# Shared expert of a two-layer AdaLN model: gate and up projections with the weights stationary, and a new order of the dense stage

## The reference

```python
logits = x @ W_gate_router
scores = jax.nn.sigmoid(logits)
_, sel = jax.lax.top_k(scores + expert_bias, 2)
top_scores = take(scores, sel); top_scores = top_scores / top_scores.sum(-1)
shared = (silu(x @ Wg_s) * (x @ Wu_s)) @ Wd_s          # x: 4096x256, Wg_s and Wu_s: 256x192, Wd_s: 192x256
h = silu(x @ Wg[e]) * (x @ Wu[e])                      # eight experts of the same size, two of them for a token
out = shared + sum over the two chosen experts of top_score * (h @ Wd[e])
```

## Time and profile before

| what | value |
| --- | --- |
| runs (us) | 916.97, 918.64, 922.68 |
| median (us) | 918.64 |
| span of the profiled execution (us) | 911.5 |
| dense stage in that execution (us from the span's start) | 338.4 to about 477 |
| PE busy over the span | 831.9 us, 91% |
| DVE, ACT, POOL busy over the span | 72%, 52%, 42% |

### The profile page before, as it was taken

The page is one execution under the profiler, slowest core; times in us unless marked ns, Lnnn a source line. Parts: engine busy times, 40 slices in busy tenths (PEclk is TensorE's granted clock), DMA queues, the critical chain, the costliest instruction groups (busy, mean ns, idle before and its releaser), DMA issues.

```text
span 911.5 us, 16937 instructions
## 1 busy us (share of the span) xinstructions
PE 831.9 (91%) x5115; PEld 744.7 (82%) x5115; DVE 652.8 (72%) x1917; ACT 474.6 (52%) x1006; POOL 379.5 (42%) x427
## 2 busy tenths in 40 slices
PE   6899999999999978889868999999698899988997
PEld 5789998987999877778758999999577788876776
DVE  3666677735567676878784676576768999888986
ACT  2443343434334338777724676466344345449883
POOL 3542200169000014564642445475678886423230
PEclk9799999989999995999998999999899999999999
DMA  9200000000000004242335445334411200000112
GB/s 306 104 1 1 2 1 1 2 1 1 1 1 1 2 22 136 89 140 89 112 112 148 126 129 179 103 112 133 128 47 47 65 29 1 1 1 24 47 47 70
DMA packets 47799, 58.31 MB, mean 64 GB/s; under 512 B 5599, under 2 KB 42848, under 8 KB 47712
## 3 DMA queue, kind: packets, MB, share of 16 engines
q1 hardware_dynamic: 39856, 39.11, 14.5%
q0 software_dynamic: 6480, 16.92, 5.1%
q10 hardware_dynamic: 1376, 1.20, 0.4%
HBM read 34.91 MB, written 23.22 MB: 64 GB/s over the span
## 4 chain that ended last, share of the span: by engine, by line
PE 32%; DVE 15%; issue 6%; ACT 5%; POOL 2%; SPq 1%; DMA 0%; DVEq 0%; ACTq 0%; POOLq 0%
PE bank L80 7%; PE bank L82 7%; PE bank L81 7%; PE bank L1701 2%; PE bank L1709 2%; PE bank L1600 1%; DVE xm L2090 1%; PE bank L1717 1%; PE bank L1721 1%; PE bank L1718 1%; PE bank L1719 1%; PE bank L1720 1%; DVE st L2026 1%; ACT spare L1211 1%; DVE hth L1415 1%
## 5 line engine op out<-in xcount | busy, mean ns | idle before, releaser
L367 ACT CAST pth<-tp 128x512 fp32r<-128x512 f32 (+3 forms) x80 | 41.7, 525 | 128.8 <-PE tp L717 127.4
L1144 POOL DMA_INDIRECT results<-row_tiles,idu x71 | 70.0, 986 | 89.0 <-ACT row_tiles L1293 75.0
L1128 POOL DMA_INDIRECT region<-row_tiles,posu x64 | 66.3, 1035 | 59.8 <-DVE posu L1399 42.7
L547 DVE TENSOR_TENSOR ptl<-tp,pth 128x512 fp32r<-128x512 f32 (+3 forms) x80 | 48.2, 607 | 54.7 <-ACT pth L367 54.6
L80 PE MATMUL cx<-vh,pth 128*128 128x256 f32 x272 | 80.6, 296 | 1.4 <-DVE ptl L547 1.2
L82 PE MATMUL cx<-vh,ptl 128*128 128x256 f32 x272 | 76.8, 282 | 0.0
L81 PE MATMUL cx<-vl,pth 128*128 128x256 f32 x272 | 76.8, 282 | 0.0
L80 PE MATMUL sc<-hh,ph 128*128 128x512 f32 (+3 forms) x160 | 61.0, 381 | 0.3
L82 PE MATMUL sc<-hh,pl 128*128 128x512 f32 (+3 forms) x160 | 58.3, 364 | 0.0
L81 PE MATMUL sc<-hl,ph 128*128 128x512 f32 (+3 forms) x160 | 58.1, 363 | 0.0
L358 ACT ACTIVATE prob<-sc,nmx 128x512 f32<-128x512 f32 (+3 forms) x80 | 49.4, 628 | 14.0 <-DVE nmx L520 14.0
(11 more groups left out here) (430 smaller groups left out, 2787.0 us busy)
## 6 DMA issues: line engine op xcount, KB each, us to landing
row_tiles<-region SPq DMA_DIRECT2D x71, 130.0 KB, 2.3
pairs_a<-results SPq DMA_DIRECT2D x10, 512.0 KB
x<-in_x SPq DMA_DIRECT2D x8, 512.0 KB, 10.7
out<-x SPq DMA_DIRECT2D x8, 512.0 KB, 2.9
pairs_b<-results SPq DMA_DIRECT2D x6, 512.0 KB, 4.9
early<-in_wmod SPq DMA_DIRECT2D x2, 768.0 KB, 4.6
early<-in_wmod SPq DMA_DIRECT2D x1, 1536.0 KB, 8.3
spare<-in_wg SPq DMA_DIRECT2D x8, 192.0 KB, 2.7
```

What stands on the lines that cost most here:

```text
L367: a_.copy(pth[:, m % 2, 0:w], tp[:, m % 2, 0:w]).then_inc(s["pt_hi"], 1)
L547: vec.tensor_tensor(ptl[:, m % 2, 0:w], tp[:, m % 2, 0:w], pth[:, m % 2, 0:w], ALU.subtract).then_inc(s["pt_lo"], 1)
L1128: g_.indirect_dma_start(region, bass.IndirectOffsetOnAxis(ap=posu[:, c, t:t + 1], axis=0), hb[:, G % HB, j], None).then_inc(scattered[G % ...
L1144: g_.indirect_dma_start(results, bass.IndirectOffsetOnAxis(ap=idu[:, j % 8:j % 8 + 1], axis=0), y[:, j % YR, 0:D], None, bounds_check=KS * ...
```

## The change

The shared expert no longer goes by tile but by group and feature-major: the gate and up weights are the stationary operand and the 512 tokens of a group stream through (`dense_up(G, m)`, three blocks m of 128 features, 6 matmuls of 512 columns each). The 192 features of gate and of up are laid out by the host as features 128 to 191 of gate and of up (block 0), features 0 to 127 of gate (block 1), the same of up (block 2); the two weight inputs become one array `wgu_s`. The gated values come out feature-major, as the down product needs them, so that `turn`, `ht_hi`, `ht_lo` and `hidden` go from this stage. In their place come, per group, two silus, two products, three copies for the high part and two subtractions, on 512 columns each; the down product (`dense_down`) keeps its 20 matmuls, in two halves of two tiles that share one PSUM bank, and the sum to x is added by halves (512 columns).

The arrays `fh` (high parts) and `fl` (low parts) have one copy each, and `act2` too. The lists of the four engines are written anew, one pass of the loop per group:

```diff
+            def gate_b(G):
+                act.wait_ge(g["up_ready"], G * 3 + 1)
+                need(act, g["lo"], G * 2 - 1)
+                a_.activation(act2[F - P:P, 1], up3[0:F - P, 0], ACT.Silu).then_inc(g["silu_done"], 1)
+            def gate_a(G):
+                act.wait_ge(g["up_ready"], G * 3 + 2)
+                need(act, g["lo"], G * 2)
+                a_.activation(act2[:, 0], up3[:, 1], ACT.Silu).then_inc(g["silu_done"], 1)
+            def hi_b(G):
+                act.wait_ge(g["product"], G * 2 + 1)
+                need(act, g["down_ready"], G * 2)
+                a_.copy(fh[F - P:P, 1], act2[F - P:P, 1]).then_inc(g["hi"], 1)
+                a_.copy(fh[0:F - P, 1], act2[F - P:P, 1]).then_inc(g["hi"], 1)
+            def hi_a(G):
+                act.wait_ge(g["product"], G * 2 + 2)
+                need(act, g["down_ready"], G * 2)
+                a_.copy(fh[:, 0], act2[:, 0]).then_inc(g["hi"], 1)
...
             for G in range(1, GROUPS + 1):
+                gate_b(G - 1)
                 if G < GROUPS:
+                    h_hi(G)
                     sigmoid(G)
+                hi_b(G - 1)
+                if G + 1 < GROUPS:
+                    z_of(G + 1)
+                gate_a(G - 1)
                 if G < GROUPS:
                     h_back(G, 0)
+                    up_weights(G + 1, G)
+                    h_back(G, 1)
+                hi_a(G - 1)
                 if G + 1 < GROUPS:
+                    h_of(G + 1)
                 if G < GROUPS:
                     down_weights(G + 1, G)
...
+            for G in range(1, GROUPS):
+                product_b(G - 1)
+                h_lo(G)
+                if G > 1:
+                    add(G - 2, 0)
+                choose(G)
+                low_b(G - 1)
+                if G > 1:
+                    add(G - 2, 1)
+                weigh(G)
+                low_up_weights(G + 1, G)
+                product_a(G - 1)
+                rank_of(G)
+                low_a(G - 1)
+                low_down_weights(G + 1, G)
...
+            def dense_up(G, m):
+                need(pe, g["product"], G * 2 - 1 if m == 0 else G * 2)
+                for e in range(KC):
+                    last = three(nc.tensor, up3[:, m], gsh[:, e, q], gsl[:, e, q], hh[G % 2][:, e], hl[G % 2][:, e], e == 0, e == KC - 1)
+                last.then_inc(g["up_ready"], 1)
+            def dense_down(G, i):
+                pe.wait_ge(g["lo"], (G + 1) * 2)
+                pe.wait_ge(g["hi"], (G + 1) * 3)
+                need(pe, g["x_added"], G * 2 + i)
...
+            for G in range(1, GROUPS):
+                dense_up(G - 1, 0)
+                logits(G)
+                if G > 1:
+                    dense_down(G - 2, 0)
+                dense_up(G - 1, 1)
+                if G > 1:
+                    dense_down(G - 2, 1)
+                turn_h(G, 0)
+                dense_up(G - 1, 2)
+                turn_h(G, 1)
+                if G + 1 < GROUPS:
+                    turn_z(G + 1)
+                count(G)
```

More of the change, by code:

```diff
@@ L1310, in _ @@
                 for j in of_pair(p):
-                    silu(N1 + j)
+                    silu(j)
                 if 1 <= p < PAIRS - 1:
@@ L1435, in _ @@
             weigh(0)
+            rank_of(0)
             low_up_weights(1, 0)
             low_down_weights(1, 0)
[L1438 to L1493, removed]
@@ new lines, in _ @@
+            flat = lambda a: a.rearrange("p t e -> p (t e)")
+            v.wait_ge(s["const2"], 2)
+            c_.link(vec.tensor_copy(fillu[:], base[:]))
+            v.sem_inc(s["fill_at"], 1)
+            c_.link(vec.tensor_tensor(n_e[:], base[:], ebase[:], ALU.subtract))
+            product_b(GROUPS - 1)
+            c_.link(vec.tensor_tensor(there, n_e[:].unsqueeze(1).to_broadcast([P, TPE, E]),
+                                      m128[:].unsqueeze(2).to_broadcast([P, TPE, E]), ALU.is_gt))
@@ new lines, in _ @@
+            c_.link(vec.tensor_tensor_scan(flat(order), plain[:, 0:1].to_broadcast([P, E * TPE]), flat(there), 0.0, ALU.mult, ALU.add))
+            c_.link(vec.tensor_tensor(order, order, there, ALU.mult))
+            add(GROUPS - 2, 0)
+            low_b(GROUPS - 1)
+            c_.link(vec.tensor_scalar(mine, order, own[:, 0:1], None, ALU.is_equal))
+            vec.tensor_reduce(in_e, mine.rearrange("p t e -> p e t"), AX.X, ALU.add)
+            c_.link(vec.tensor_reduce(in_t, mine, AX.X, ALU.add))
@@ L1498, in slot_lo @@
+            product_a(GROUPS - 1)
+            add(GROUPS - 2, 1)
+            v.wait_ge(s["slots_known"], 1)
+            vec.tensor_copy(exf[:], lg[:, 0:SLOTS])
+            vec.tensor_copy(exu[:], lg[:, 0:SLOTS])
+            c_.link(vec.tensor_scalar(colf[:], lg[:, SLOTS:2 * SLOTS], -1.0, float(USED), ALU.mult, ALU.add))
+            vec.tensor_copy(colu[:], colf[:]).then_inc(s["tabled"], 1)
+            low_a(GROUPS - 1)
+            add(GROUPS - 1, 0)
+            add(GROUPS - 1, 1)
             def slot_lo(p):
@@ L1622, in count @@
                 last.then_inc(s["counted"], 1)
-            def up(n, half, stat, e):
-                need(pe, s["hid_done"], n - 1)
-                wh, wl = (gsh, gsl) if e is None else (expert_w(guh, e), expert_w(gul, e))
-                for c in range(KC):
-                    last = three(nc.tensor, gu[:, n % 2, 0:2 * F], hh[half][:, c, stat], hl[half][:, c, stat], wh[:, c], wl[:, c],
-                                 c == 0, c == KC - 1)
-                last.then_inc(s["gu_ready"], 1)
@@ new lines, in dense_down @@
+            def dense_down(G, i):
+                pe.wait_ge(g["lo"], (G + 1) * 2)
+                pe.wait_ge(g["hi"], (G + 1) * 3)
+                need(pe, g["x_added"], G * 2 + i)
+                mm, wh, wl = nc.tensor.matmul, dsh[:, G // GPB], dsl[:, G // GPB]
+                for j in (2 * i, 2 * i + 1):
+                    q, out = slice(j * P, (j + 1) * P), dp[:, (j % 2) * D:(j % 2 + 1) * D]
+                    mm(out, fh[:, 0, q], wh[:, 0], start=True, stop=False)
+                    mm(out, fh[:, 0, q], wl[:, 0], start=False, stop=False)
+                    mm(out, fl[:, q], wh[:, 0], start=False, stop=False)
+                    mm(out, fh[:, 1, q], wh[:, 1], start=False, stop=False)
+                    last = mm(out, fh[:, 1, q], wl[:, 1], start=False, stop=True)
+                last.then_inc(g["down_ready"], 1)
@@ L1691, in _ @@
+            dense_up(GROUPS - 1, 0)
+            dense_down(GROUPS - 2, 0)
+            dense_up(GROUPS - 1, 1)
+            dense_up(GROUPS - 1, 2)
+            dense_down(GROUPS - 2, 1)
+            pe.wait_ge(s["spread"], 1)
+            nc.tensor.matmul(lg[:, 0:2 * SLOTS], plain[:], spread.rearrange("p i j -> p (i j)"), start=True,
+                             stop=True).then_inc(s["slots_known"], 1)
+            dense_down(GROUPS - 1, 0)
+            dense_down(GROUPS - 1, 1)
             pe.wait_ge(s["tabled"], 1)
@@ L1692, in _, with up @@
             pe.wait_ge(s["w_lo"], 2 * (E + 1))
-            pe.wait_ge(s["x_added"], N1)
+            pe.wait_ge(g["x_added"], 2 * GROUPS)
+            def up(n, stat, e):
+                need(pe, s["hid_done"], n - 1)
+                wh, wl = expert_w(guh, e), expert_w(gul, e)
+                for c in range(KC):
+                    last = three(nc.tensor, gu[:, n % 2, 0:2 * F], hh[0][:, c, stat], hl[0][:, c, stat], wh[:, c], wl[:, c],
+                                 c == 0, c == KC - 1)
+                last.then_inc(s["gu_ready"], 1)
```

180 lines of the change are left out of this document (69 added, 111 removed).

## The result

The changed kernel is slower. Four runs took 937.2, 956.7, 956.8 and 940.0 us; four of the kernel before, on the same chip, 914.5 to 922.7. The ratio is 1.0207, with a 95% interval from 1.0142 to 1.0272, and 918.64 times that is 937.7 us. Runs of one kernel fall into quicker and slower ones, here 2% apart: every ratio is made from the quicker ones, the stretches from the profiled run, which is a quicker one except in e4 and e6. The profiled execution took 937.2 with a span of 935.4, which is 23.9 more than the 911.5 of before.

The account below looks back on a forecast made before the run. The prediction took a ring of waits through PE, ACT and DVE to bound the kernel. At full clock 1.6 - 2.5 + 0.5 = -0.4 us, plus 6.0 for the clock, gave +5.6 on 918.64: 924 us, range 912 to 937.

Parts of the forecast that it names:

- rival 1: Dense stage: the clock stays low through the ring's PE part, 3.3 us a period, 19.8 in six, 938 us; chance 0.20.
- the period of 16 to 17: Dense stage: sign that the forecast is right, 16 to 17 us from one group's logits to the next.
- PE's smaller sum of work: PE in the dense stage: sign that its work falls, by about 1 us a period.
- `fillu` between 463 and 472 us: End of the dense stage: sign that `fillu` comes between 463 and 472 us on the timeline.
- The ring at full clock: Dense stage: longest chain of waits through ACT, DVE and PE, 15.65 us a period, 0.31 more than before.
- The last logits to `fillu`: End of the dense stage: this stretch takes 13.8 us instead of 16.28, a change of -2.5.
- PE's idle time: Dense stage: PE has nothing to do for some 3.8 us a period, from its third up block until `h_back`.
- The clock term: PE's part of the ring: falls to 1.2 GHz cost 1.0 us a period, +6.0 in six passes.
- The end: From `fillu` to the slots stage: the last add falls 15.2 us behind `fillu`, for which 0.5 us is added.
- Rival 2: Dense stage: the clock costs nothing on the ring, -0.4 us, so 918 us; chance 0.20.
- rival 3: Dense stage: ACT alone sets the period, about 12.2 us, so 901 us; chance 0.06.
- Rival 4: ACT in the dense stage: a drain follows each table load on the ring, 6 x 1.38 us, so 932 us; chance 0.02.

Follow-up runs that it names:

- e4: Changed kernel with ACT's `z_of` ahead of `hi_b` and DVE's `product_a` ahead of `low_up_weights`; four runs of 908.6, 922.6, 925.5 and 2016.9 us, no ratio.
- e6: e4 with the last group's work reordered, its last downs in their own bank, PE's register reads and first turn before its wait; 911.38 us, ratio 0.9822.
- e5: e1 with 8 more unused matmuls on PE between the first up block and the logits; 923.83 us, ratio 1.0044.
- e7: e6 with 12 unused matmuls on PE behind the third up block; 907.54 us, ratio 0.9799.
- e1: Changed kernel with 28 unused matmuls of 256 columns on PE behind the third up block in each period; 937.94 us, ratio 1.0155.
- e8: Kernel before the change with PE's register reads and first turn ahead of the wait for the last add; 922.75 us, ratio 1.0027.

## Why the prediction was right in its ring and short in its time

The range ended at 937, and the time, 937.7, lies at that end; the point, 924, is some 14 us too low, and "within 1%" was the wrong one of the three outcomes. What came is the price of rival 1, 938, to which 0.20 was given, and its sign, a period of 18 and more. Three signs of the forecast did not come: the period of 16 to 17, PE's smaller sum of work (it grew by 4.8 us) and `fillu` between 463 and 472 us (484.98). That the time still met the end of the range is in part luck: the clock cost 16 us in five periods, not the 19.8 in six of rival 1, and a late end of 4.2, for which no rival had a price, makes up for it. Step by step:

- **The ring at full clock held.** 15.65 summed, 15.99 in e5. Its members held too: the waits of `hi_b`, `hi_a` and `low_up_weights` are there with the releasers named, 2.1 and 1.0 us for ACT's two in e5 (2.2 and 1.2 forecast), and with both of them taken away (e4, e7) the period falls to 12.8, near the 12.2 estimated for ACT alone. In the kernel after itself, at the low clock, the ring does not run over `h_of`.
- **The last logits to `fillu` held**: 13.8 summed, 14.1 measured. So did PE's idle time, 3.8 against 4.0.
- **The clock term failed: 1.0 a period, measured 3.24** (19.23 less 15.99). The step was "the fall after logits comes in about half of the periods (0.8) and the one after the idle time mostly meets `dense_up(G, 0)`, which has 1 us of slack (0.2)". Neither half came so. No fall of the kernel after begins behind logits; each period has one that begins behind the idle time, of 3.4 and 13.7 us in turn. The short one ends ahead of the logits, and the period that they begin is 17.3 to 17.5, since the next long fall starts before it is over; the long one runs over the first up block, the logits and the downs, and that period takes 20.2 to 20.7. The slack of `dense_up(G, 0)` did not hold either: PE comes to the logits 0.7 us after `h_of` behind the short fall and 1.4 in the long one. Filling the first gap takes the period from 19.23 to 17.58 (e1, four periods), filling the second as well to 15.99 (e5): together they are the 3.24, but since other falls come in e1, 1.65 and 1.6 are no measure of the two halves. The prediction took the length of a fall, 3.3, from falls behind logits and behind 2.4 us of idle time, and applied it to idle times of 4. That was the mistake. The trace of before had a gap of 4.94 us, with a fall of 10.2, and the prediction did not use it. The profiled execution lies 18.3 us above the forecast (23.9 less 5.6); five periods at 2.24 too little are 11.2 of them, five at 0.34 of the ring 1.7, the end 3.7; the other lines of the table give the remaining 1.7.
- **The end failed: +0.5, measured +4.2.** The step was "the last add falls 15.2 us behind `fillu`"; it ended 18.0 behind. The last group is a chain (silu, product, high and low parts, downs, add, downs, add) and its members stand behind DVE's table of experts, behind downs that wait for adds in a shared bank, and at the low clock: the last matmuls start 0.21 apart instead of 0.12. To these comes the 1.78 of register reads behind the last wait. e6 changes the order, the bank and the reads together and gets the 4.2 back; how it divides among them was not tried one by one. In the kernel before the same reads cost 0.3 at most (e8).
- **Rival 1 was right in its price and only half in its place.** It asked for a fall within 2 us of most logits and one more on the first up block, 3.3 in all. In the kernel after it is the fall behind the idle time alone, every second time four times as long; one behind the logits comes as soon as the other is kept away (e1), and goes when the idle time ahead of the logits is filled too (e5).
- **Rival 2** (the clock costs nothing) and **rival 3** (ACT alone) did not come, but both can be made: e5 is nearly the first, e7 the second.
- **Rival 4 fell.** The silu starts at 405.97, 0.01 after the load at 404.68 has ended. The drain of 1.38 us that the Trainium skill, "ScalarE: Activation LUTs", section "What ACT_TABLE_LOAD costs", adds to a load is not to be seen here, and the measurement decides.

What stays open is why a fall lasts 3.4 us in one period and 13.7 in another, and whether the 2.3 us ahead of the first logits have to do with the change at all; they lie within what that stretch varies by.

## What to carry to other kernels

Cutting PE's work in a ring of several engines makes room for idle time on PE, and that idle time has a price of its own: take the length of the clock's falls from a stretch with gaps as long as the new ones, or give both ends to the range; here the beginning of the dense stage was one. Two waits on such a ring are tried one by one and together: one order alone took 1.9 us off the mean period and the other nothing, both took it from 19.2 to 14.9, and to 12.8 where the clock is up. At the end of a stage, put what needs no result (register reads, the first turn) ahead of the last wait, and count the last group's chain against the transfer that used to hide it.

## What the runs showed of the hardware that was not expected

Matmuls whose results nothing reads made the changed kernel quicker. 36 a period of 256 columns kept the granted clock at 1.00 over 80 us and took the ratio from 1.0207 to 1.0044. The Trainium skill, "TensorE: Matmul & The Clock Gate", section "Part 1: The HAM clock gate (the "warmup" mystery)", says that activity is what releases the low clock; e1, e5 and e7 agree.

The falls themselves were less regular than expected. After 4.0 us of idle time the clock stayed at 1.2 GHz for 3.4 us or for 13.7, in alternation, though PE was busy in all of the 13.7; after 2.2 us in e4, in which PE was busy for 0.26, for 13.7 again; and behind 16 matmuls of 8 columns, with 28 unused matmuls placed earlier and 0.84 us of idle time just ahead, for 3.4 in each of four periods and for 6.8 in the fifth (e1). With 8 more unused matmuls in the place of that 0.84 us no fall came (e5).
